# A decoder layer's gated delta rule: outputs and z made transposed, the row factor applied behind the output projection, the inverse dealt out by other costs

## What is computed

```
mixed = silu(causal_conv4(x @ w_qkv)); q, k, v = split(mixed)   # 16 q/k heads, 32 v heads, of 128
z = x @ w_z                                                     # 32 heads of 128
g = -exp(A_log) * softplus(a + dt_bias);  beta = sigmoid(b)
q, k = l2norm(q) * 128 ** -0.5, l2norm(k)
for each token:                                                 # per v head, state Sm of 128 x 128
    Sm = Sm * exp(g);  delta = (v - k @ Sm) * beta
    Sm = Sm + outer(k, delta);  o = q @ Sm
og = o * silu(z)
on = og * rsqrt(mean(og * og) + eps) * norm_w                   # mean over a head's 128
y = on @ w_out                                                  # over 32 heads x 128
```

## Time and profile before

| | |
|---|---|
| median of 3 runs | 2197.31 us (2196.64 to 2201.7) |
| the profiled execution | 2197.97 us, its span 2196.2 us, mean granted TensorE clock 0.969 |
| TensorE busy | 2018.6 us (92% of the span), weight loads 1681.6 (77%) |
| VectorE busy | 1723.7 us (78%) |
| ScalarE busy | 1497.9 us (68%) |
| GpSimd busy | 893.3 us (41%) |
| DMA | 161.56 MB, mean 74 GB/s |

### The profile page before, as it was taken

How to read it: one execution, slowest core, us unless ns; L and a number is a source line. 1 busy time by engine, 2 the same in 40 slices (tenths; PEclk the granted TensorE clock), 3 DMA queues, 4 the chain that set the end, 5 groups by cost and what they waited for, 6 DMA issues and landing times.

```text
span 2196.2 us, 49295 instructions
## 1 busy us (share of the span) xinstructions
PE 2018.6 (92%) x18636; PEld 1681.6 (77%) x18636; DVE 1723.7 (78%) x2944; ACT 1497.9 (68%) x3523; POOL 893.3 (41%) x714
## 2 busy tenths in 40 slices
PE   4648999999999999999999999998878899999998
PEld 3437888888888888888888888887765567666676
DVE  6789798898988889898898988975236777767665
ACT  4536877778777787777878778765667666665632
POOL 1623454454454544544544545432343213322232
PEclk8869999999999999999999999998989999999999
DMA  3422323323233323323233232211342022222232
GB/s 79 96 70 50 81 57 69 83 55 67 63 74 71 68 65 67 74 65 75 64 61 79 63 70 71 42 49 48 87 148 87 1 97 73 82 96 97 83 129 87
DMA packets 274633, 161.56 MB, mean 74 GB/s; under 512 B 209352, under 2 KB 246752, under 8 KB 269280
## 3 DMA queue, kind: packets, MB, share of 16 engines
q1 hardware_dynamic: 274400, 158.41, 27.6%
HBM read 122.43 MB, written 35.91 MB: 72 GB/s over the span
## 4 chain that ended last, share of the span: by engine, by line
issue 35%; POOL 27%; PE 22%; DVE 9%; ACT 4%; DMA 2%; SPq 1%; POOLq 0%; DVEq 0%; ACTq 0%
POOL Q L557 5%; POOL SM L579 5%; POOL EB L495 5%; PE ps L1735 4%; POOL SZ L581 4%; PE ps L1351 3%; POOL EB L499 3%; PE ps L1352 2%; PE ps L1353 2%; POOL WL L473 2%; POOL SM L587 2%; ACT SC L860 2%; PE ps L1647 1%; PE ps L1656 1%; PE ps L1484 1%
## 5 line engine op out<-in xcount | busy, mean ns | idle before, releaser
L913 DVE SCALAR_TENSOR_TENSOR A<-ps,CW,A 128x508 f32<-128x508 f32 (+2 forms) x768 | 517.1, 735 | 62.7 <-ACT A L676 59.9
L574 POOL TENSOR_SCALAR SM<-SM 128x8 f32<-128x8 f32 x64 | 12.7, 198 | 746.8 <-ACT DL L695 746.8
L1351 PE MATMUL ps<-XH,WH 128*128 128x512 f32 x512 | 223.2, 436 | 31.9 <-DVE A L913 31.0
L1484 PE MATMUL ps<-WO,DL 128*128 128x256 f32 x1008 | 232.7, 384 | 19.0 <-ACT DL L682 11.6
L1484 PEld LDWEIGHTS ps<-WO,DL 128*128 128x128 f32 x1008 | 193.3, 193 | 47.9 <-ACT DL L682 13.4
L1353 PE MATMUL ps<-XH,WL 128*128 128x512 f32 x512 | 208.1, 407 | 0.0
L1352 PE MATMUL ps<-XL,WH 128*128 128x512 f32 x512 | 207.5, 405 | 0.0
L695 ACT ACTIVATE DL<-SZ 128x128 f32<-128x128 f32 x512 | 152.9, 300 | 59.4 <-issue 32.6
L1131 DVE TENSOR_TENSOR SZ<-SZ,ps 128x512 f32<-128x512 f32 x128 | 86.6, 687 | 128.4 <-PE ps L1520 126.9
L860 ACT ACTIVATE SC<-ps,A 128x128 f32<-128x128 f32 x512 | 142.2, 387 | 51.3 <-DVE A L1256 50.7
L1116 DVE TENSOR_TENSOR BP<-ps,EB 128x512 f32<-128x512 f32 x256 | 158.4, 682 | 2.6 <-ACT EB L667 2.6
(11 more groups left out here) (223 smaller groups left out, 5530.7 us busy)
## 6 DMA issues: line engine op xcount, KB each, us to landing
EB<-decay_rows SPq DMA_DIRECT2D x128, 256.0 KB, 4.6
WE<-expert_halves SPq DMA_DIRECT2D x32, 1024.0 KB, 5.1
x_blocks<-BP SPq DMA_DIRECT2D x256, 32.0 KB, 1.7
X<-x_blocks SPq DMA_DIRECT2D x16, 512.0 KB, 5.8
tt_blocks<-TI SPq DMA_DIRECT2D x16, 512.0 KB, 2.6
tn_blocks<-TM SPq DMA_DIRECT2D x16, 512.0 KB, 2.6
TTF<-tt_blocks SPq DMA_DIRECT2D x256, 32.0 KB, 1.9
expert_halves<-BP SPq DMA_DIRECT2D x8, 1024.0 KB, 5.5
```

Of the source, the lines that this page charges most:

```text
L913: dve.scalar_tensor_tensor(acc, ps(i, 0, [[128, 4], [1, 128 - s]]), at(CW, tile * 4 + 3 - s, [[1, 1]]), acc, ALU.mult, ALU.add).then_inc(s ...
L1351: pe.matmul(out, sa, ma, start=(kt == 0), stop=False)
L1484: t = pe.matmul(ps(7 - i, b * 256, [[1, 256]]), at(on_buf(k), (4 * i + 2 * b + v) * 128, [[1, 128]]), at(WO, v * 256, [[1, 256]]), start=( ...
```

## The change

**Transposed outputs.** `outputs` swaps its operands, so o comes as [value, token], and its two halves are told apart by pairs of sequences. `z_proj` goes by v head instead of by sequences, as `proj` does for q, k and v: six matmuls of 512 columns instead of twelve of 256. The gated outputs in SZ then are already what `out_proj` needs as weights: `on_tr` and `on_T` go.

**The factor.** The mean of squares now runs over partitions. `squares` are two operations of 512 columns into DL; `og_sums`, eight matmuls with the selection matrix PICK as `norms` has, sums them into bank 2; ScalarE copies the row to RRW, `og_sums_tr` transposes it, VectorE's `mean_squares` and GpSimd's `pow` make the factor. Since it differs between v heads, `out_proj(k, v, i)` keeps them apart: v = 0 in banks 4 and 5, ahead of u2, v = 1 in banks 6 and 7, behind kq_mm. ScalarE's `y_head` copies v = 0 out with the factor as its scale (four operations, into DL); VectorE's `y_head` multiplies v = 1 and adds it to Y (four operations of 256 columns); GpSimd's `y_add` adds DL to Y. `delta`, which writes DL, waits for that (`y_add`). GpSimd no longer scales SZ.

**TensorE's order.** `norms` and `og_sums` stand ahead of u1, `norms_tr` ahead of `v_proj(vn, 0)`.

**The inverse.** Products cost 150 + 1.05 n, sums 180 + 1.72 n; the pumps have rooms of 800, 3300, 700 (or 50000) and 2900; it is put under way right behind `norm_sums`.

**Its way.** ScalarE's copy to TM stands behind v_silu. `store_tn` is a function of its own. In the tick n % 4 = 3 SP issues `store_x` and `load_rows` first, then `store_t`, `store_tn`, `load_ta`, `load_x`, `load_tt`; in other ticks `load_tt` stands last too.

The diff, cut to its core and moved left by eight columns:

```diff
+def o_bank(k, b, v):
+    return 6 + v if k >= NSTEP - 2 else 4 + 2 * v + b // 2
...
+        def store_tn(j):
             sp.wait_ge(sem["tn"], j + 1)
...
-            if n % 4 == 0 and 4 <= n <= NSTEP:
-                load_x(n // 4 - 1)
...
-                store_t(wn // 4)
-            if 0 <= wn < NSTEP:
+            if 0 <= wn < NSTEP and wn % 4:
                 load_ta(wn)
-                load_tt(wn)
+            if wn == 0:
+                store_t(0)
+                store_tn(0)
+                load_ta(0)
+                load_tt(0)
             if n < NSTEP:
                 store_x(n)
             if n + 3 < NSTEP:
                 load_rows(n + 3)
+            if 0 < wn < NSTEP and wn % 4 == 0:
+                store_t(wn // 4)
+                store_tn(wn // 4)
+                load_ta(wn)
+            if n < NSTEP and n % 4 == 3:
+                load_x(n // 4)
+            if 0 < wn < NSTEP:
+                load_tt(wn)
...
+        def y_add(k):
+            yo = at(Y, 4 * (k % 4) * 256, full)
+            pool.wait_ge(sem["y_v0"], 4 * k + 4)
+            if k >= NSTEP - 2:
+                pool.wait_ge(sem["y_v1"], 4 * k + 4)
+            elif k >= 4:
+                pool.wait_ge(sem["y_v1"], 4 * (k - 4) + 4)
+            pool.tensor_tensor(yo, yo, at(y_buf(k), 0, full), ALU.add).then_inc(sem["y_add"], 1)
...
+            if 0 <= k < NSTEP:
+                pool.wait_ge(sem["xs"], k + 1)
+                if k >= 2:
+                    pool.wait_ge(sem["y_v0"], 4 * (k - 1))
+                    pool.wait_ge(sem["y_v1"], 4 * (k - 1))
+                pool.tensor_tensor(at(SM, C_RR + 8 * (k % 2), [[1, 8]]), at(SM, C_XS, [[1, 8]]), at(SM, C_MH, [[1, 8]]),
+                                   ALU.pow).then_inc(sem["rr"], 1)
...
-            if s3:
...
-                pool.wait_ge(sem["ss"], 2 * m + 2)
-                pool.tensor_scalar(xs, at(SM, C_SS, [[1, 8]]), 1.0 / 128, 1.0, ALU.mult, ALU.mult).then_inc(sem["xs"], 1)
...
-                pool.tensor_tensor(xs2, xs2, at(SM, C_NQ + (m % RING) * 4, [[1, 4], [0, 2]]), ALU.add).then_inc(sem["xs"], 1)
-                pool.wait_ge(sem["xs"], 2 * m + 2)
-                pool.tensor_tensor(rr, xs, at(SM, C_MH, [[1, 8]]), ALU.pow).then_inc(sem["rr"], 1)
-                pool.wait_ge(sem["rr"], m + 1)
-                pool.tensor_tensor(szp, szp, at(SM, C_RR, [[1, 8], [0, 128]]), ALU.mult).then_inc(sem["on"], 1)
...
+        def y_head(k):
+            act.wait_ge(sem["rr"], k + 1)
...
+            for b in range(4):
+                act.wait_ge(sem["out_mm"], o_count(k, b, 0))
+                act.activation(at(y_buf(k), b * 256, [[1, 256]]), ps(o_bank(k, b, 0), b % 2 * 256, [[1, 256]]), ACT.Copy,
+                               scale=at(SM, C_RR + 8 * (k % 2) + 2 * b, [[1, 1]])).then_inc(sem["y_v0"], 1)
...
         def squares(m, i):
...
-            for pr in range(4 * i, 4 * i + 4):
-                t = act.activation(at(DL, pr * 128, [[1, 128]]), at(SZ, (m % 2) * 1024 + pr * 128, [[1, 128]]),
-                                   ACT.Square, accum_out=at(SM, C_SS + pr, [[1, 1]]))
-            t.then_inc(sem["ss"], 1)
+            act.wait_ge(sem["o_mm"], 2 * m + 1 + i)
+            act.activation(at(DL, i * 512, [[256, 2], [128, 2], [1, 128]]), by_batch(SZ, (m % 2) * 1024, i),
+                           ACT.Square).then_inc(sem["og_sq"], 1)
...
+            if s4:
+                act.wait_ge(sem["og_mm"], k + 1)
+                if k:
+                    act.wait_ge(sem["og_tr"], k)
+                act.activation(at(RRW, 0, [[1, 128]]), ps(2, 0, [[1, 128]]), ACT.Copy).then_inc(sem["og_row"], 1)
...
+            if s1 and s4:
+                y_head(k)
...
-            if s4 and k < NSTEP - 1:
-                on_T(k, 0)
-            if 0 <= wn < NSTEP and wn % 4 == 0:
-                act.wait_ge(sem["inv"], INV_OPS * (wn // 4 + 1))
-                act.activation(at(TM, 0, [[1, 32], [32, 32]]), at(TI, 0, [[32, 32], [1, 32]]), ACT.Copy).then_inc(sem["tn"], 1)
-            if s4 and k < NSTEP - 1:
-                on_T(k, 1)
...
+            if 0 <= wn < NSTEP and wn % 4 == 0:
+                act.wait_ge(sem["inv"], INV_OPS * (wn // 4 + 1))
+                act.activation(at(TM, 0, [[1, 32], [32, 32]]), at(TI, 0, [[32, 32], [1, 32]]), ACT.Copy).then_inc(sem["tn"], 1)
             if s3:
                 if s4:
-                    act.wait_ge(sem["out_mm"], 2 * k + 2 if m < NSTEP - 1 else 2 * k)
+                    act.wait_ge(sem["og_mm"], k + 1)
+                if 0 <= k < NSTEP - 2:
+                    act.wait_ge(sem["y_add"], k + 1)
                 for i in range(2):
                     act.wait_ge(sem["d_mm"], 2 * m + 1 + i)
...
+        def mult_ns(n):
+            return 150 + 1.05 * n
+        def sum_ns(n):
+            return 180 + 1.72 * n
...
+        def y_head(k):
+            dve.wait_ge(sem["rr"], k + 1)
...
+            for b in range(4):
+                yo = y_row(4 * (k % 4) + b)
+                dve.wait_ge(sem["out_mm"], o_count(k, b, 1))
+                dve.scalar_tensor_tensor(yo, ps(o_bank(k, b, 1), b % 2 * 256, [[1, 256]]), at(SM, C_RR + 8 * (k % 2) + 2 * b + 1, [[1, 1]]),
+                                         yo, ALU.mult, ALU.add).then_inc(sem["y_v1"], 1)
...
         def gate(m, i):
-            dve.wait_ge(sem["z_silu"], 2 * m + 1 + i)
+            z = at(SZ, (m % 2) * 1024 + i * 256, [[512, 2], [1, 256]])
+            dve.wait_ge(sem["z_silu"], 2 * m + 2)
             dve.wait_ge(sem["o_mm"], 2 * m + 1 + i)
-            dve.tensor_tensor(z_half(m, i), z_half(m, i), ps(6 + i), ALU.mult).then_inc(sem["og"], 1)
+            dve.tensor_tensor(z, z, ps(6 + i, 0, [[256, 2], [1, 256]]), ALU.mult).then_inc(sem["og"], 1)
+        def mean_squares(k):
+            dve.wait_ge(sem["og_tr"], k + 1)
...
+            dve.scalar_tensor_tensor(at(SM, C_XS, [[2, 4], [1, 2]]), ps(2, 128, [[32, 4], [1, 2]]), 1.0 / 128,
+                                     at(SM, C_NQ + (k % RING) * 4, [[1, 4], [0, 2]]), ALU.mult,
+                                     ALU.add).then_inc(sem["xs"], 1)
...
+            pump(800)
+            if s4:
+                mean_squares(k)
             if n % 4 == 0 and 4 <= n <= NSTEP:
                 norm_sums(n // 4 - 1)
-            pump(2500)
-            pump(1560)
+                if n >= EARLY:
+                    under_way.append(inverse(n // 4 - 1))
+            pump(3300 if EARLY <= n < NSTEP else 0 if n == NSTEP else 5000 // rate)
...
-            pump(500)
-            if n % 4 == 3:
-                pump(50000)
+            pump(50000 if n % 4 == 3 else 700)
             if s4 and k < NSTEP - 2:
-                y_add(k, 0)
-            if s4 and k < NSTEP - 2:
-                y_add(k, 1)
-            pump(2000)
+                y_head(k)
+            pump(2900)
...
+        def og_sums(k):
+            pe.wait_ge(sem["og_sq"], 2 * k + 2)
...
+            for v in range(2):
+                for b in range(4):
+                    t = pe.matmul(ps(2, 0, [[1, 128]], 32 * b, 32), at(PICK, 31 - v, [[1, 32]]),
+                                  at(DL, (2 * b + v) * 128, [[1, 128]]), start=(v == 0), stop=(v == 1))
+            t.then_inc(sem["og_mm"], 1)
...
+        def og_sums_tr(k):
+            pe.wait_ge(sem["og_row"], k + 1)
+            if k:
+                pe.wait_ge(sem["xs"], k)
+            pe.transpose(ps(2, 128, [[1, 128]]), at(RRW, 0, [[1, 128]]), idn).then_inc(sem["og_tr"], 1)
...
+        def z_proj(m, v):
+            if m % 4 == 0 and v == 0:
+                pe.wait_ge(sem["lo_z"], m // 4 + 1)
+            pe.wait_ge(sem["vv"], 4 * m + 2 + 2 * v)
+            proj(4 + v, W_Z + 128 * v, m % 4).then_inc(sem["z_mm"], 1)
...
+        def out_proj(k, v, i):
+            if k % 4 == 0 and v == 0 and i == 0:
...
+            pe.wait_ge(sem["og"], 2 * k + 1 + i)
...
+            elif v:
+                pe.wait_ge(sem["tt128_sb"], k + 2)
                 pe.wait_ge(sem["u2_sb"], k + 3)
             else:
-                pe.wait_ge(sem["tt128_sb"], k + 2)
-            for b in range(2):
-                for v in range(2):
-                    t = pe.matmul(ps(7 - i, b * 256, [[1, 256]]), at(on_buf(k), (4 * i + 2 * b + v) * 128, [[1, 128]]),
-                                  at(WO, v * 256, [[1, 256]]), start=(v == 0), stop=(v == 1))
+                pe.wait_ge(sem["z_silu"], 2 * (k + 1) + 1 + i)
+            for b in (2 * i, 2 * i + 1):
+                t = pe.matmul(ps(o_bank(k, b, v), b % 2 * 256, [[1, 256]]), at(SZ, (k % 2) * 1024 + v * 512 + b * 128, [[1, 128]]),
+                              at(WO, v * 256, [[1, 256]]), start=True, stop=True)
...
+            pe.wait_ge(sem["z_silu"], 2 * m + 1 + i)
+            if 0 < m < NSTEP - 1:
+                pe.wait_ge(sem["y_v0"], 4 * (m - 1) + 2 + 2 * i)
             pe.wait_ge(sem["vv"], 4 * m + 2 + 2 * i)
...
                 pr = 4 * i + j
```

(18 more changed lines are left out.)

199 lines of the change are left out of this document (93 added, 106 removed).

## The result

The changed kernel takes 2296.31 us (median of 4 runs, 2291.52 to 2299.27), the kernel before 2198.51: a ratio of 1.0441, 95% interval [1.0416, 1.0466]. Forecast were 2215, and 2153 to 2246 for eight cases in ten. The profiled execution's span is 2297.4 us, 101.2 more than before's 2196.2.

The account below looks back on a forecast made before the run. The prediction took TensorE (PE) as the bound, busy 91.23 of 92.84 us a cycle. Terms -55.5 + 16.8 + 47.6 + 11 - 20 + 17 = +16.9 on 2197.97 us gave 2215 us, range 2153 to 2246.

Parts of the forecast that it names:

- PE's work: On TensorE in every tick: on_tr and half of z_proj's matmuls go, og_sums and og_sums_tr come; net 0.61 us less, -33.6 us.
- on_tr's and gate's waits gone: On TensorE once a cycle each: on_tr's wait for SZ (-14.4 us) and u1's for gate (-7.5 us) go.
- v_tr waits for delta: Tick n % 4 = 3: ScalarE's moved copy to TM makes delta late, a new 1.2 us wait 14 times, +16.8 us.
- u1 and t64 wait for TA and TTF: Once a cycle, inverse's stores queue behind EB, so TA lands late: 3.2 us, plus 0.2 for TTF, 14 times, +47.6 us.
- og_sums waits for VectorE: After the tick n % 4 = 0, VectorE is late and og_sums waits 0.85 us, 13 times, +11 us.
- the clock in the steady part: u1's wait may pull TensorE's clock down: 2.45 us lost in half of 14 cycles, +17 us, bounds 0 and +34.
- tail: From n = 64: out_proj's wait for on_T goes, less PE work, last inverse starts earlier; -20 us, between -8 and -30.
- ring order: Skill's rule that each DMA engine consumes descriptors in ring order; by it alone u1 waits the full 2.7 to 3.7 us.
- Rival 1: TA in time: tn_blocks isn't held up by EB, TA lands by S + 26.4; 2153 us, chance 0.30.
- VectorE: VectorE's work grows from 81.4 to about 84 us of an 88.7 us cycle; fits unevenly, 1.15 us late at n % 4 = 0.
- Rival 3: VectorE becomes the bound: inverse not spread as meant, y_head slower, every tick 0.6 us longer; +33, 2248 us, chance 0.08.
- The sign: The whole kernel gets slower, by +16.9 us; chances slower 0.53, same 0.15, faster 0.32.

Follow-up runs that it names:

- eb_last: The changed kernel with the two EB loads issued last in the ticks n % 4 = 3: 2293.5 us, 1.042 of the kernel before.
- l_eb_last: l_only with the two EB loads of the tick n % 4 = 3 issued last: 2229.9 us, 1.014 of the kernel before.
- i_only: The kernel before with only the inverse's new costs, pumps and start: 2277.1 us, 1.037 of the kernel before.
- t_only: The kernel before with only the transposed outputs; copy to TM, loads and the inverse's costs and pumps as before: 2279.7 us, ratio 1.039.
- l_only: The kernel before with only the copy to TM and SP's order of loads moved as in the change: 2282.8 us, ratio 1.039.
- t_dve_y: Transposed outputs alone, GpSimd's decay behind sq and its work waiting for v_tap 1, VectorE adding both heads, two pumps resized: 2290.1 us, 1.040 of before.

## Why the prediction was wrong

By its terms, in the profiled executions (forecast; measured):

| term | forecast | measured |
|---|---|---|
| PE's work | -33.6 | -16.9 |
| on_tr's and gate's waits gone | -21.9 | -20.9 |
| v_tr waits for delta | +16.8 | +8.0 |
| u1 and t64 wait for TA and TTF | +47.6 | +48.1 |
| og_sums waits for VectorE | +11 | +9.2 |
| kq_proj waits for v_tap 3 | 0 | +17.5 |
| the clock in the steady part | +17 | +45.6 |
| tail | -20 | +14.4 |
| start, and everything behind | 0 | -3.8 |
| sum | +16.9 | +101.2 |

**What bounds the kernel** was read rightly: PE sets the pace, and the change lost by making it wait.

**The sum.** The forecast lacked 84 us. Four terms failed: the tail (34 us more than forecast), the clock (29), kq_proj's wait for v_tap 3, which had no term (17.5), and PE's work (17). The others were 13 us too dear, 9 of them v_tr's wait, 0.6 us a cycle instead of 1.2. The 11 us of og_sums were added although the prediction calls them hidden where u1's wait is long; 9.2 came all the same.

**TA.** Forecast 3.2 us a cycle for TA, measured 3.5, by the mechanism named, and eb_last and l_eb_last show it: without EB ahead it is 0.3. That the sentence on ring order of the Trainium skill, DMA: Bandwidth & Descriptors, section Queues, rings and completion order, was weighed as speaking against the change was right. Rival 1 was wrong in its price all the same: with TA in time it gave 2153 us, and the run with TA in time took 2293.5. The prediction's sum treated the waits as additive, while they stand in one tick in parallel; TA's wait covered VectorE's lateness, and appears as VectorE's wait once TA's is gone.

**VectorE** is the step whose mechanism failed, and the reason that the parts can't be saved one by one. The prediction counted its work at the lengths of before (84 us of 88.7), said that it "fits, but not evenly", let VectorE be 1.15 us late in the tick n % 4 = 0, and gave kq_proj no wait; in the changed kernel kq_proj waits 17.5 us in five cycles, in eb_last 3.9 us a cycle in eight of nine. Two things were missed. mean_squares stands ahead of everything VectorE does next and waits for a transpose behind u1, so VectorE can't use the time in which PE waits: 6.18 us idle. And the inverse's products don't have a fixed length: begun while GpSimd is at one of its large operations they take up to five times as long in the mean of a group, and the new start puts them there. The rows for this stood in the trace of before, in the groups by form: of two products with the same shape one took 1151 ns in the mean and the other 693, and the shortest of the first took 692.

```profile
L978 DVE TENSOR_TENSOR TM<-X,TI 128x512 f32<-128x512 f32 x16 | 18.4, 1151 | 0.6
...
L990 DVE TENSOR_TENSOR TM<-TI,UT 128x512 f32<-128x512 f32 x16 | 11.1, 693 | 0.5
```

ScalarE and GpSimd outside the named places were priced at "Nothing", as GpSimd has 2 us to spare before delta needs y_add; it is busy for only 45 of 92.8 us a cycle, but what matters is beside what they lie. Rival 3, VectorE as the bound, was right in kind, at +33 and 0.08; alone i_only costs 79.

**The clock.** Forecast 2.45 us in half of the cycles, taken from one wait of 2.47 us in the tail. It fell in 12 of 13 cycles, four of them twice, and cost 3.5 us a cycle, the low stretches being 3.4 to 10.2 us long. The term's mechanism was right, its size wrong by 2.7 times: no row stood behind "half of 14 cycles", and the price of a fall came from a single one. That the waits so far, 1.03 us at most, left the clock at 1.00 said nothing of one of 3.5.

**PE's work.** z_proj's halves take 1.56 and 1.49 us at the full clock (t_only) instead of the 1.43 forecast from kq_proj, so 0.18 us are saved and not 0.38; og_sums_tr takes 0.20 and not 0.12. 0.33 us a tick, not 0.61, which is the -16.9 over 52 ticks. That time between unlike groups of matmuls was left out is a likely reason, not shown.

**The tail.** Forecast -20, measured +14.4, the largest miss of all; TensorE's idle time there went from 17.1 to 32.3 us. out_proj's waits for on_T did go (9.1 us), and u1's for gate (6.0), but og_sums waits for the squares, 11.5 us in six places, and these for gate behind pumps that have double rooms there:

```profile
1577.44 0.87 PE L1464 MATMUL ps<-DL,PICK 128*32 128x128 f32 x12 [5.82 <-ACT DL L733]
```

v_tr waits 12.7 us in seven ticks for delta, which in five of them waits for y_add, and out_proj once 7.3 us for WO, until 1700.81 us. The prediction took away the old waits and named nothing that is late next. No run was made on the tail, so these are readings of the trace.

**The sign** was right, the size was not: 98 us where 17 was said. The sign rests on TA's term, which l_only bears out, so it isn't luck; that the terms of the sum nearly cancelled hid how much hung on each.

## What to carry to other kernels

When work is moved in time on an engine, ask beside what on the other engines it then runs: VectorE's products of two SBUF tensors should not begin while GpSimd is at a large operation on SBUF, and this is seen by setting an instruction's shortest time beside its mean. Moving GpSimd's work beside VectorE's operations on PSUM avoids it, if what waits for GpSimd can bear it. An operation put first in an engine's order hands its wait to all behind it, so look for what it waits for before counting the engine's free time. Parts of a change that hurt the same tick don't add up, and undoing one of them gives little: price each on the kernel before.

## What the runs showed of the hardware

- A VectorE TENSOR_TENSOR with both inputs in SBUF, 0.23 us alone for 64 columns, took up to 2.31 us beside GpSimd (changed kernel). Begun while one large GpSimd operation was running it was slowed in 255 of 272 cases, begun before it in 0 of 284; in the second case GpSimd took longer, 2.21 to 2.97 us instead of 1.90 for the scaling of SZ. `pow` on 8 or 16 columns slowed none of 1863; sums (0 of 1342) and taps and products of BP, which have one input in PSUM (0 of 7844), weren't slowed at all.
- In the changed kernel waits of TensorE of 2.2 to 4.7 us, once or twice in 100, came with 3.4 to 10.2 us at 1.2 GHz in 12 of 13 cycles (in one, with waits of 2.34 and 2.58 us, the clock stayed at 1.00); waits of 0.6 to 1.0 us in the kernel before left it at 1.00 in all 13 cycles. A wait's length alone doesn't decide: in t_dve_y, where none is over 1.9 us but they come in most ticks, the clock cost 34 us. What decides wasn't settled.
- A 512 KB store (tn_blocks) landed 7.6 us after its issue behind 1 MB issued in the 2.5 us ahead of it (5.6 in the median), and 2.6 us where nothing large was still under way (kernel before).
